# Laying out the operands of an eight-wide attention: one DMA for a pair of heads in place of four, and one for the rows of maxima

## The reference, cut to what matters

```
q, k, v = x @ Wq, x @ Wk, x @ Wv            # 512 x 128, 16 heads of 8
s = (q_h @ k_h.T) * scale                   # 512 x 512 per head
s = where(causal, s, -inf)                  # layers 0 and 1
out_h = softmax(s, axis=-1) @ v_h
```

## Time and profile before

| | us |
|---|---|
| median of 3 runs | 3166.05 (3158.64 to 3183.53) |
| the profiled execution | 3194.17 |
| its span, first to last instruction | 3192.4 |
| busy: PE, DVE, ACT, POOL | 2670.9, 1758.7, 1299.2, 605.6 |
| mean granted clock of TensorE | 0.82 of full speed |
| SP's DMAs from `parts` | 384, of 48 KB each |
| SP's DMAs from `nmT` | 144, of 4 KB each |

### The profile page before, as it was taken

How to read it: one execution, slowest core, us unless ns; L and a number is a source line. 1 busy time by engine, 2 the same in 40 slices (tenths; PEclk the granted TensorE clock), 3 DMA queues, 4 the chain that set the end, 5 groups by cost and what they waited for, 6 DMA issues and landing times.

```text
span 3192.4 us, 39656 instructions
## 1 busy us (share of the span) xinstructions
PE 2670.9 (84%) x13585; PEld 1357.3 (43%) x13585; DVE 1758.7 (55%) x4863; ACT 1299.2 (41%) x3060; POOL 605.6 (19%) x849
## 2 busy tenths in 40 slices
PE   4888998889988887888758988987899888888885
PEld 2233335434553585244423333353345446742363
DVE  5535446654564597633465444485356547776154
ACT  1445632353324442563424556214532344435741
POOL 0330001221101483000012200012201127720000
PEclk7688988678887998768768888977798789988776
DMA  5100001200000001100011000022001000011000
GB/s 168 23 1 1 1 1 33 50 11 21 24 24 1 1 8 41 48 1 31 18 48 22 1 1 1 1 46 47 1 20 34 14 1 1 29 46 22 1 1 7
DMA packets 37787, 67.51 MB, mean 21 GB/s; under 512 B 4873, under 2 KB 30345, under 8 KB 35722
## 3 DMA queue, kind: packets, MB, share of 16 engines
q1 hardware_dynamic: 37010, 63.69, 7.8%
q10 hardware_dynamic: 576, 1.29, 0.1%
HBM read 44.45 MB, written 1.05 MB: 14 GB/s over the span
## 4 chain that ended last, share of the span: by engine, by line
PE 64%; DVE 17%; ACT 8%; issue 6%; SPq 1%; POOL 1%; DMA 1%; ACTq 0%; POOLq 0%; DVEq 0%
PE psum L567 5%; PE psum L989 4%; PE psum L2149 4%; PE psum L1000 3%; PE psum L557 3%; DVE floor_s L2248 3%; PE psum L973 2%; PE psum L1524 2%; PE psum L815 2%; PE psum L740 2%; PE psum L1354 2%; PE psum L539 2%; PE psum L1816 2%; DVE mx_s L705 2%; PE psum L1802 2%
## 5 line engine op out<-in xcount | busy, mean ns | idle before, releaser
L641 ACT ACTIVATE PT_s<-psum 128x512 f32<-128x512 f32 (+3 forms) x768 | 341.9, 496 | 283.7 <-PE psum L557 282.2
L386 POOL TENSOR_SCALAR ve<-mv 128x4 f32<-128x4 f32 x48 | 13.6, 282 | 1649.3 <-DVE mv L376 1649.1
L539 PE MATMUL psum<-KS_s,QS_s 48*128 48x512 bf16 (+3 forms) x768 | 214.4, 416 | 113.8 <-DMA QS_s<-parts_s 56.3
L2175 POOL TENSOR_TENSOR buffer<-sim_s 128x1024 f32<-128x1024 f32 x128 | 271.8, 2138 | 176.1 <-DVE floor_s L2248 94.3
L702 DVE CUSTOM_DVE_ANT_0 rest_s<-psum,packed_early 128x128 f32<-128x128 f32 (+3 forms) x512 | 225.8, 487 | 89.6 <-PE psum L539 86.7
L567 PE MATMUL psum<-PT_s,vaug 128*9 128x512 f32 (+3 forms) x1536 | 199.7, 599 | 52.9 <-POOL PT_s L675 35.9
L557 PE MATMUL psum<-QS_s,KS_s 51*128 51x512 bf16 (+3 forms) x768 | 208.7, 391 | 34.7 <-ACT PT_s L641 21.1
L675 POOL TENSOR_SCALAR_AFFINE_SELECT PT_s<-PT_s 128x128 f32<-128x128 f32 x512 | 148.7, 301 | 392.2 <-ACT PT_s L641 387.6
L2208 ACT ACTIVATE above_s<-buffer,below_s 128x1024 f32<-128x1024 f32 x128 | 145.4, 1149 | 135.6 <-PE psum L2149 91.7
L1037 ACT ACTIVATE PT_s<-psum 128x512 f32<-128x512 f32 (+1 forms) x224 | 121.1, 592 | 170.0 <-PE psum L991 169.9
L705 DVE TENSOR_REDUCE mx_s<-psum 128x1 f32<-128x512 f32 x256 | 159.9, 682 | 50.0 <-PE psum L539 49.4
(11 more groups left out here) (441 smaller groups left out, 5132.4 us busy)
## 6 DMA issues: line engine op xcount, KB each, us to landing
buffer<-packed_experts SPq DMA_DIRECT2D x36, 384.0 KB, 3.5
KS_s<-parts_s SPq DMA_DIRECT2D x192, 48.0 KB
QS_s<-parts_s SPq DMA_DIRECT2D x192, 48.0 KB
buffer<-packed_moe SPq DMA_DIRECT2D x4, 2048.0 KB, 8.0
buffer<-packed_cross SPq DMA_DIRECT2D x4, 2048.0 KB, 7.8
buffer<-packed_product SPq DMA_DIRECT2D x4, 1024.0 KB, 4.8
packed_early<-packed_early SPq DMA_DIRECT2D x1, 2654.0 KB
QS_s<-nmT_s SPq DMA_DIRECT2D x144, 4.0 KB
```

Of the source, the lines that this page charges most:

```text
L539: pe.matmul(bank[n % 4][:, 0:n_keys], QS[stack(h), h // 2, j * P:(j + 1) * P], KS[stack(h), h // 2, 0:n_keys], start=True, stop=True, tile ...
L641: a.activation(PT[:, u // 4 % 2, i, q0_of(c):T], bank[u % 3][:, q0_of(c):T], ACT.Exp, scale=scale).then_inc(exp_done.sem, 1)
L2175: g.tensor_tensor(fs[:, n % 2], m[:, 0, :].unsqueeze(2).to_broadcast([P, NK, NK]), m[:, 1, :].unsqueeze(1).to_broadcast([P, NK, NK]), ALU. ...
```

## The change

`parts` gets eight slots for each dimension, of which six are filled as before, with q and k of a slot side by side. One slice of 16 of its partitions (a pair of heads) then holds 128 rows of q and of k in the order in which the stacks want them, and `stacks` is one tile in which `QS` and `KS` are two halves. So a pair of heads takes one DMA of 128 partitions x 2 x 512, and the stage 8 in place of 32.

The two slots that are left over, 16 rows of each head, are filled by POOL at the start of the stage: zeros for q, ones for k. This does away with the two DMAs of ones. The matmuls of both kinds go over all 64 rows of a head. The rows of maxima go into the seventh row of every group of 16 rows of `QS` (`QS[6::16]`; the slice steps over four partitions a head), three with the parts of the maxima and one with zeros, so that one DMA with a stride of 16 partitions does a half of the heads; for this `nm` and `nmT` have room for four parts, and POOL clears `nm` too. The three memsets wait for the stage's `xT_ready`, and SP (before the first DMA) and DVE (before it splits the maxima) wait for them.

`rest` and `parts` together are now 4 KB longer per partition than `PT`, which lies over them, and the stacks are moved behind them.

```diff
-SLOTS = 6
+SLOTS, FILLED = 8, 6
+MAX_STEP = 16
-    parts = s.tile("parts", [P, 2, SLOTS, T], BF16)
+    parts = s.tile("parts", [P, SLOTS, 2, T], BF16)
+    after_parts = s.at
     s.at = under_PT
     PT = s.tile("PT", [P, 2, 4, T])
-    QS = s.tile("QS", [P, H // 2, T], BF16)
-    KS = s.tile("KS", [P, H // 2, T], BF16)
+    s.at = max(s.at, after_parts)
+    stacks = s.tile("stacks", [P, 2, H // 2, T], BF16)
+    QS, KS = stacks[:, 0], stacks[:, 1]
-    nm = s.tile("nm", [P, 2, TJ, 2, 3, H // 4])
-    nmT = s.tile("nmT", [3 * H // 2, 2, T], BF16)
+    nm = s.tile("nm", [P, 2, TJ, 2, 4, H // 4])
+    nmT = s.tile("nmT", [2 * H, 2, T], BF16)
...
-                pe.matmul(bank[n % 4][:, 0:n_keys], QS[stack(h), h // 2, j * P:(j + 1) * P], KS[stack(h), h // 2, 0:n_keys],
+                pe.matmul(bank[n % 4][:, 0:n_keys], QS[half(h), h // 2, j * P:(j + 1) * P], KS[half(h), h // 2, 0:n_keys],
...
     def sync(sp):
         yield T1 - 2
-        for ready in (keys_split(4), queries_split(4), keys_repeated(2), queries_repeated(2)):
+        for ready in (keys_split(4), queries_split(4), keys_repeated(2), queries_repeated(2), pads_set(3)):
             sp.wait_ge(*ready)
         for loaded, (first, last) in zip(pairs_loaded, PAIR_GROUPS):
-            for h in range(2 * first, 2 * last):
-                for q, to in ((1, KS), (0, QS)):
-                    sp.dma_start(to[stack(h), h // 2, :], parts[h * HD8:(h + 1) * HD8, q, :, :]).then_inc(loaded.sem, 16)
-        for o in range(2):
-            row = 64 * o + SLOTS * HD8
-            sp.dma_start(KS[row:row + 3].rearrange("p i t -> p (i t)"), s.ones_rows).then_inc(ones_loaded.sem, 16)
+            for i in range(first, last):
+                sp.dma_start(stacks[:, :, i, :], parts[2 * HD8 * i:2 * HD8 * (i + 1)]).then_inc(loaded.sem, 16)
         for t, kind, u in plan:
             yield t
             if kind == "spread":
                 sp.wait_ge(*max_copied(u + 1))
-                for o in range(2):
-                    for w in range(3):
-                        row = 64 * o + SLOTS * HD8 + w
-                        at = 12 * o + 4 * w
-                        sp.dma_start(QS[row:row + 1, 4 * u:4 * u + 4, :], nmT[at:at + 4, u, :]).then_inc((first_rows, last_rows)[u].sem, 16)
+                sp.dma_start(QS[FILLED::MAX_STEP, 4 * u:4 * u + 4, :], nmT[:, u, :]).then_inc((first_rows, last_rows)[u].sem, 16)
...
     def gpsimd(g_):
+        yield 0
+        g_.wait_ge(*xT_ready)
+        g_.memset(parts[:, FILLED:SLOTS, 0, :], 0.0).then_inc(pads_set.sem, 1)
+        g_.memset(parts[:, FILLED:SLOTS, 1, :], 1.0).then_inc(pads_set.sem, 1)
+        g_.memset(nm[:], 0.0).then_inc(pads_set.sem, 1)
         yield T1 - 6
         g_.wait_ge(*(roped if rope else qk_biased)(1))
...
                 v.wait_ge(*scores_read(H * TJ // 2 * (u + 1)))
+                v.wait_ge(*pads_set(3))
```

More of the change, by code:

```diff
@@ L38, in host_constants @@
     c["ident"] = np.eye(P, dtype=np.float32)
-    c["ones_rows"] = np.ones((3, HEADS8 // 2 * T), np.float32).astype(mybir.dt.np(BF16))
     selmax = np.zeros((P, HEADS8 // 2, P), np.float32)
@@ L456, in attention8 @@
      scores_read, chain, max_split, max_turned, max_copied, first_rows, last_rows, st_ready, exp_done, exp_masked, pv_done, out_copied, out_turned,
[L457 removed]
+     att_ready, att_turned, attT_ready, branch_ready, pads_set, *pairs_loaded) = s.signals(
         qk_projected=2, v_projected=1 if wv is not None else 0, qk_biased=2, rotated=2 if rope else 0, rope_chain=4 if rope else 0,
         roped=2 if rope else 0, keys_split=4, queries_split=4, keys_repeated=2, queries_repeated=2, v_ready=1, ring_ready=len(ring) - 1, scores_read=H * TJ,
[L460 removed]
+        chain=12 + G, max_split=2, max_turned=2, max_copied=2, first_rows=16, last_rows=16, st_ready=H * KC, exp_done=H * KC,
         exp_masked=H * KC if causal else 0, pv_done=G * KC, out_copied=G, out_turned=G, att_ready=G,
         att_turned=1 if wo is not None else 0, attT_ready=1 if wo is not None else 0, branch_ready=1 if wo is not None else 0,
[L463 removed]
+        pads_set=3, **{f"pairs_loaded{n}": 16 * (b - a) for n, (a, b) in enumerate(PAIR_GROUPS)})
     s.new_stage()
@@ L488, in q0_of @@
         return c * P if causal else 0
-    def stack(h, more=0):
-        return slice(64 * (h % 2), 64 * (h % 2) + SLOTS * HD8 + more)
     counted = {step: n + 1 for n, step in enumerate(step for step in ring if step[0] != "turn")}
@@ L536, in tensor @@
                     if u == 2 * TJ * first:
-                        pe.wait_ge(*loaded(64 * (last - first)))
+                        pe.wait_ge(*loaded(16 * (last - first)))
                 n_keys = (j + 1) * P if causal else T
-                pe.matmul(bank[n % 4][:, 0:n_keys], QS[stack(h), h // 2, j * P:(j + 1) * P], KS[stack(h), h // 2, 0:n_keys],
+                pe.matmul(bank[n % 4][:, 0:n_keys], QS[half(h), h // 2, j * P:(j + 1) * P], KS[half(h), h // 2, 0:n_keys],
                           start=True, stop=True, tile_position=(64 * (h % 2), 0)).then_inc(ring_ready.sem, 1)
@@ L549, in tensor @@
                 if u == 0:
-                    pe.wait_ge(*ones_loaded(32))
-                    pe.wait_ge(*first_rows(96))
+                    pe.wait_ge(*first_rows(16))
                     pe.wait_ge(*scores_read(H * TJ))
                 if h == H // 2 and c == 0:
-                    pe.wait_ge(*last_rows(96))
+                    pe.wait_ge(*last_rows(16))
                 if u >= 3:
                     pe.wait_ge(*exp_done(u - 2))
-                pe.matmul(bank[u % 3][:, q0_of(c):T], KS[stack(h, 3), h // 2, c * P:(c + 1) * P], QS[stack(h, 3), h // 2, q0_of(c):T],
+                pe.matmul(bank[u % 3][:, q0_of(c):T], KS[half(h), h // 2, c * P:(c + 1) * P], QS[half(h), h // 2, q0_of(c):T],
                           start=True, stop=True, tile_position=(64 * (h % 2), 0)).then_inc(st_ready.sem, 1)
@@ L628, in scalar @@
                 a.wait_ge(*split(2 * n + 1))
-                to = parts[:, q, MORE_SLOTS[name][n], :]
-                a.copy(to, parts[:, q, FIRST_SLOT[name][n]:FIRST_SLOT[name][n] + 1, :].to_broadcast(to.shape)).then_inc(repeated.sem, 1)
+                to = parts[:, MORE_SLOTS[name][n], q, :]
+                a.copy(to, parts[:, FIRST_SLOT[name][n]:FIRST_SLOT[name][n] + 1, q, :].to_broadcast(to.shape)).then_inc(repeated.sem, 1)
         for t, kind, u in plan:
@@ L634, in scalar @@
                 a.wait_ge(*max_turned(u + 1))
-                a.copy(nmT[:, u, :], turn_bank(u)[0:3 * H // 2, :]).then_inc(max_copied.sem, 1)
+                a.copy(nmT[:, u, :], turn_bank(u)[0:2 * H, :]).then_inc(max_copied.sem, 1)
             elif kind == "exp":
@@ L652, in split_up @@
         whole, left = qk[:, q, :], rest[:, q, :]
-        first, second, third = (parts[:, q, n, :] for n in FIRST_SLOT["qk"[q]])
+        first, second, third = (parts[:, n, q, :] for n in FIRST_SLOT["qk"[q]])
         eng.tensor_copy(first, whole).then_inc(done.sem, 1)
@@ L2447, in program @@
         for name, arr in t["constants"].items():
-            if name == "ones_rows":
-                continue
             k.w[name] = sb("c_" + name, list(arr.shape), arr.dtype)
@@ L2482, in program @@
             s.moe, s.product, s.cross3 = (views(s.buffer, places[group]) for group in ("moe", "product", "cross3"))
[L2483 removed]
+            s.experts = t["experts"]
             streams.append(s)
```

6 lines of the change are left out of this document (1 added, 5 removed).

## The result

| | kernel before | changed kernel |
|---|---|---|
| median on the same chip, us | 3171.67 (4 runs) | 3137.12 (3130.58 to 3141.08, 4 runs) |
| ratio, 95% interval | | 0.989 [0.9844, 0.9936] |
| median in a second, longer comparison, us | 3179.64 (29 runs) | 3132.32 (4 runs) |
| its ratio, 95% interval | | 0.986 [0.9838, 0.9882] |
| profiled execution, and its span, us | 3194.17, 3192.4 | 3141.08, 3139.4 |

The change makes the kernel 1.1 to 1.4% faster, 35 to 47 us. The forecast was 16 us. The time of the first comparison lies within the range given (3122 to 3180), and so does that of the second; the direction is right, and the forecast gain is under half of what came. No change beyond 1% was thought the likeliest (0.75); what came is over 1% faster, which had a chance of 0.20.

A forecast was written before the change was run, and what follows sets the result against it. PE was taken to wait for layout DMAs, pair 0's in all 12 attentions. Landing 12 plus first attention 4.7 less POOL's 1 made 15.7 us, from the 3166.05 median to 3150.4 us; range 3122 to 3180.

The forecast's parts named there:

- 0.76 came with other work in the mix: Argument against a rising clock: the score stretch with granted clock 0.76, against 0.61 elsewhere, also held other work.
- the clock's case: Rival: shorter gaps and more rows lift PE's clock in ten score stretches, 40 us; 3110 us in all, chance 0.12.
- Landing of pair 0: First heads' layout in all 12 attentions: one DMA brings SP's start to first score from 5.3 to 4.3 us.
- DMA pieces on the chain of about 3.3 us: Sign expected in the profile after: chain pieces from the new DMAs this long, with no row of SP before them.
- No gain: Rival: DMA as slow as at worst, nothing for pair 0, 3.3 us in the first attention; 3164 us, chance 0.16.
- the best rate: Rival: 16 engines keep 0.056 us a piece, 2.0 us gained for each pair 0; 3137 us, chance 0.15.
- 8 engines: Rival: the new DMA stays on 8 engines and pair 0 lands 0.6 us later; 3176 us, chance 0.03.
- The first attention: Pair 4's scores there wait for DVE and no longer for SP's 32 DMAs: 4.7 us gained beyond pair 0.
- The other DMAs: Ones and spread DMAs leave SP, the bytes grow by a third; all hidden, costed at nothing.
- The memsets: Three on POOL at each stage's start, 2.75 us together, hidden except in layer 3.
- Layer 3: POOL's step waits behind the memsets in two stages: 0.5 us lost in each, 1 us in all.
- The rival of a slower kernel by POOL: Memsets take 5.4 us and delay splits, selects and layer 3, 25 us lost; 3174 us, chance 0.11.

The follow-up runs named there:

- the keys first: Changed kernel with pair 0's DMA in two halves, the keys' sent before the queries are waited for; ratio 0.9829 to the kernel before.
- 48 rows in the first scores alone: Changed kernel with only the queries-by-keys matmuls, from which the maxima are read, over 48 of 64 rows; ratio 0.9934 to the kernel before.

## Why the prediction was right or wrong

The direction and the time are right, and the mechanism is right for a third of the gain. The step that failed is the one on the matmuls: "The rows go from 48 or 51 to 64, the columns stay: I cost this at nothing, since the length of these matmuls in the rows goes by columns." At a given clock it does (1.04 us for four of 512 columns over 48 rows and over 64); the clock did not stay. Back at 48 rows with all else as changed, 0.0098 of 3170 us is 31 us, two thirds of the whole gain, and the mean clock of the timed executions falls from 0.847 to 0.828. The prediction named this as a rival ("a third more rows at work may lift it") at a chance of 0.12, priced at 40 us, which is near the 31. Its own sign of being wrong, "if the granted clock of the score stretches leaves 0.6", came: 0.84 in the second attention. It was weighed down by "0.76 came with other work in the mix", and that was the wrong row to argue from: the sum had no term for it although its size, if it came, was over twice that of everything else. The Trainium skill ("TensorE: Matmul & The Clock Gate", section "What's actually happening") says that activity of the array releases the clock and that the lower level is the default. The trace of before agrees in that the clock was down to 0.50 while PE idled, though with 56 rows, with the keys first and with 48 rows in the first scores alone it was still 1.00 from 36 to 41 us of the same idle time. From 32 to 64 rows the clock of the four stretches rose from 0.56 to 0.87 while PE's busy share of them fell from 0.90 to 0.82, so the busy time alone doesn't account for it.

That the time fell within the range is partly luck. The range leaves out the clock's case, which was priced at 3110 together with the forecast's other gains. That case came, smaller than priced, and the kernel before measured 6 to 14 us above the 3166.05 from which the range was reckoned. The ratio of the longer comparison on 3166.05 would give 3122, the very edge.

What was left for the rest of the change is 0.9958 at 48 rows, 13 us less, with an interval of 6 to 20. The forecast for the DMAs and POOL together was 15.7, right within what these runs can tell.

- Landing of pair 0, forecast 5.3 to 4.3 us, 12 us in all. Measured 5.3 to 4.6 or 4.7, 8 us in all: right in kind, a third too much. The transfer was right (16 engines, 0.097 us a piece for 0.10, 1.55 us for 1.6). The rest was forecast at 2.6 us and is 4.5 less 1.55, 2.95. It isn't SP's issue, which took 0.60 where I had 0.9; it lies between issue and landing, and no run here splits it further. The sign "DMA pieces on the chain of about 3.3 us" doesn't follow from the forecast's own sum: a piece runs from the DMA's start on SP, so it should have been 4.2, and it was 4.5. "No gain", "the best rate" and "8 engines" are ruled out by the same rows.
- The first attention, forecast 4.7 beyond pair 0. From SP's start to its start in the second attention it was 57.9 us (36.36 to 94.28) and is 52.05 (36.93 to 88.98): 5.9 us, of which 0.65 is pair 0's, so 5.2. Right, and for the reason given: the scores of pair 4 wait for DVE and no longer for a DMA. The first score comes at 41.61 and not 40.7, since SP started 0.6 later in this execution and the landing gained 0.35 less.
- The other DMAs at nothing. SP's row shows 1.5 us a DMA for "0.8 to 1.2", with others in flight; eight take 11.8 us for 23 before, and nobody waits for them. Right in result.
- The memsets, forecast 2.75 us, with bounds 0.3 and 5.4: they took 2.1. Layer 3 was to lose 0.5 us twice. From the norm's last step on POOL (L388), ahead of the memsets, to PE's step it was 12.96 us (1189.95 to the 1202.91 of the earlier trace rows) and is 13.12 (1159.68 to 1172.80), and in the second such place 13.42 both times. The fifth attention's first score is at 1196.15 for 1226.88, 30.7 sooner where PE's step is 30.1 sooner, and 0.65 of that is the landing. So at most 0.2 us was lost. The rival of a slower kernel by POOL is out. That they cost nothing in the other ten stages isn't shown: doubled, they cost 14 us, with an interval wide enough for 3.
- The level: the profiled execution of before lies 15 to 28 us above its medians and that of after 4 above its own. To forecast a difference and not a level was right; of the 53 us between the profiled executions only 35 to 47 belong to the change.

## What to carry to other kernels

Where the granted clock of a stretch is near 0.6 although PE is busy for four fifths of it, an edit that adds rows to its matmuls is not free and not neutral: price it by the rows of the trace at both clocks, and give it a term. Padding a contraction from 48 to 64 rows was worth 31 us in 3170, more than the DMAs it was made for; but it came only together with them, and with the old 32 DMAs the same rows brought no time. And where a stage's start waits for one transfer, split that one by what is ready first: halving pair 0's DMA alone, keys ahead of queries, brought another 10 us, give or take 8.
